# A transformer layer on one core: its last attention sequence, the step to the MLP, and the MLP's chain from bank to bank are rewritten

## The reference

```
cond = silu(c) @ wc.T + bc                    # split: sh1 sc1 g1 sh2 sc2 g2, one row of each per sequence
h = ln(x) * (1 + sc1) + sh1
q = h @ wq.T  (16 heads of 32)   k, v = h @ wk.T, h @ wv.T  (4 groups of 32)
a = softmax(q @ k.T / sqrt(32));  x = x + g1 * ((a @ v) @ wo.T)
h = ln(x) * (1 + sc2) + sh2
x = x + g2 * (gelu(h @ w1.T + b1) @ w2.T + b2)   # w1: 2048 x 512
```

## Time and profile before

| | us |
|---|---|
| three timed runs | 1500.55, 1500.60, 1503.28; median 1500.6 |
| profiled execution, its own time | 1506.23 |
| its span, first to last instruction | 1504.5 |
| mean granted clock of TensorE | 0.984 of full |
| busy in the span: TensorE, VectorE, ScalarE, GpSimd | 1447.9, 800.1, 621.3, 577.0 |

### The profile page before, as it was taken

The page is one execution under the profiler, slowest core; times in us unless marked ns, Lnnn a source line. Parts: engine busy times, 40 slices in busy tenths (PEclk is TensorE's granted clock), DMA queues, the critical chain, the costliest instruction groups (busy, mean ns, idle before and its releaser), DMA issues. The chain is left out here.

```text
span 1504.5 us, 19118 instructions
## 1 busy us (share of the span) xinstructions
PE 1447.9 (96%) x6989; PEld 1048.7 (70%) x6989; DVE 800.1 (53%) x1360; ACT 621.3 (41%) x1118; POOL 577.0 (38%) x224
## 2 busy tenths in 40 slices
PE   6899999999999999999799999999999999999996
PEld 5655666656666566655378878787887878878785
DVE  6877777776777677776334432424224242332421
ACT  6376657585766667575333212121121122112110
POOL 1067587776778586877200020202002020120202
PEclk9999999999999999999899999999999999999998
DMA  8232422323232324221342220200102010010100
GB/s 296 61 82 53 111 55 82 98 80 115 82 108 78 103 54 124 66 83 39 105 149 83 77 64 1 91 0 28 63 0 91 0 64 27 28 63 0 63 1 28
DMA packets 68388, 105.15 MB, mean 70 GB/s; under 512 B 10504, under 2 KB 19736, under 8 KB 68320
## 3 DMA queue, kind: packets, MB, share of 16 engines
q1 hardware_dynamic: 68320, 104.27, 22.6%
HBM read 55.44 MB, written 16.81 MB: 48 GB/s over the span
## 5 line engine op out<-in xcount | busy, mean ns | idle before, releaser
L824 DVE TENSOR_REDUCE neg_max<-row_bank 128x1 f32<-128x512 f32 x512 | 337.6, 683 | 146.8 <-PE row_bank L1062 142.3
L1500 PE MATMUL acc<-w_t,hidden 128*128 128x512 f32 x1536 | 370.8, 391 | 7.7 <-DVE hidden L1417 7.7
L1490 PE MATMUL up<-h,w_t 128*128 128x512 f32 x1536 | 371.2, 392 | 0.0
L668 ACT ACTIVATE probs<-key_bank 128x512 f32<-128x512 f32 x512 | 299.6, 597 | 169.1 <-PE key_bank L1075 163.8
L1500 PEld LDWEIGHTS acc<-w_t,hidden 128*128 128x128 f32 x1536 | 287.3, 188 | 69.9 <-DVE hidden L1417 10.7
L1490 PEld LDWEIGHTS up<-h,w_t 128*128 128x128 f32 x1536 | 287.6, 188 | 58.7
L1415 DVE CAST hidden<-gelu_full 128x512 fp32r<-128x512 f32 x128 | 67.4, 527 | 443.8 <-ACT gelu_full L1361 442.2
L1361 ACT ACTIVATE gelu_full<-up,bias_cols 128x512 f32<-128x512 f32 x128 | 88.3, 690 | 515.3 <-PE up L1490 515.3
L547 POOL TENSOR_TENSOR probs_sum<-probs_sum,probs 128x2048 f32<-128x2048 f32 x62 | 285.4, 4603 | 15.6 <-ACT probs L668 9.3
L1075 PE MATMUL key_bank<-q_stack,k_stack 98*128 98x512 f32 x512 | 221.3, 435 | 4.2 <-ACT probs L668 3.9
L1318 POOL TENSOR_TENSOR y<-y,gate_now 128x512 f32<-128x512 f32 x32 | 47.4, 1482 | 454.9 <-DVE y L1425 454.9
(11 more groups left out here) (133 smaller groups left out, 1066.0 us busy)
## 6 DMA issues: line engine op xcount, KB each, us to landing
q_stack<-spare SPq DMA_DIRECT2D x384, 64.0 KB, 2.0
xa<-in_x_dram SPq DMA_DIRECT2D x8, 1024.0 KB, 9.4
resid<-in_x_dram SPq DMA_DIRECT2D x8, 1024.0 KB, 7.0
x_scratch<-resid SPq DMA_DIRECT2D x8, 1024.0 KB, 4.5
xa<-x_scratch SPq DMA_DIRECT2D x8, 1024.0 KB, 5.8
spare<-in_L_cond_w_dram SPq DMA_DIRECT2D x32, 256.0 KB, 3.0
resid<-x_scratch SPq DMA_DIRECT2D x8, 1024.0 KB, 6.8
out_dram<-y SPq DMA_DIRECT2D x8, 1024.0 KB, 4.2
```

Source lines behind the costliest of these rows:

```text
L668: nc.scalar.activation(probs[kt][:, r, :], key_bank[r % 2][:, :], ACT.Exp).then_inc(exp_done, 1)
L824: nc.vector.tensor_reduce(out=neg_max[:, g % 2, i:i + 1], in_=row_bank[(g + i) % 2][:, :], op=ALU.max, axis=AX.X, negate=True).then_inc(ro ...
L1490: last = nc.tensor.matmul(up[j % 2][:, :], w1_t[i][:, kt, j * P:j * P + P], h[k][:, kt, :], start=(kt == 0 and n == 0), stop=(kt == KD - 1 ...
L1500: last = nc.tensor.matmul(acc[tt][:, :], hidden[j % 2][i][:, tt * P:tt * P + P], w2_t[k][:, j, :], start=(j == 0 and n == 0), stop=(j == N ...
```

## The change

1. **One block for both halves.** `attention` and `mlp` return their functions for each engine, and one block calls first the one, then the other. wq_t and wo_t move in memory.
2. **A table of its own for the last sequence** (`LAST_FILL`): O1d, O2 and O3 later, T0 to T3 at the ends of groups 0 and 3.
3. **Sums of the last sequence:** two additions in place of three; `sums` takes the fourth tile by a second set of matmuls. The groups' heads go into wq_t, which is free by then.
4. **The end of attention:** sums right after the products with V; O2 and O3 in the two `row_bank`s, all four tiles first for three groups, with weight tiles 0 and 1 turned between them (into `acc` banks, which are the former `key_bank`s); then the fourth group of all four. `up_product(0)` waits for two gates, `down_product(0)` for all.
5. **MLP in place:** Gelu and the modulation write back into their PSUM banks; ScalarE makes the high part, VectorE only the low one. up(j) now waits for the split of hidden j - 2, not its Gelu.
6. **The output:** VectorE multiplies `acc` by the gate; GpSimd has b2 times the gate added to the residual ahead of time, and adds that once. In the last sequence VectorE adds tiles 2 and 3 itself, and each tile is stored by its own transfer of 256 KB.
7. **The front:** B3 ahead of r0.

```diff
+WEIGHTS_AHEAD = 2
+LAST_FILL = {
+    (0, 0): ("Q3a", "Q3bc", "", "Q3d"),   (0, 1): ("", "", "VT", ""),
+    (0, 2): ("", "", "", ""),             (0, 3): ("", "", "T0", ""),
+    (1, 0): ("O0a", "O0b", "", "O0c"),    (1, 1): ("", "", "O0d", ""),
+    (1, 2): ("", "O1ab", "", ""),         (1, 3): ("O1c", "", "", ""),
+    (2, 0): ("", "O1d", "O2a", ""),       (2, 1): ("", "", "O2b", ""),
+    (2, 2): ("O2c", "O2d", "", ""),       (2, 3): ("", "O3a", "", "O3b"),
+    (3, 0): ("", "O3cd", "", "T1 T2"),    (3, 1): ("", "", "", ""),
+    (3, 2): ("T3", "", "", ""),           (3, 3): ("", "", "", ""),
+}
-... Wo.3 Mc3.1 Mc3.2 Mc3.3 r0 r1 Wc4.0 Q1a B3 r2 r3 Wc4.1 Mc4.0 r4 ...
+... Wo.3 Mc3.1 Mc3.2 Mc3.3 B3 r0 r1 Wc4.0 Q1a r2 r3 Wc4.1 Mc4.0 r4 ...
...
+def adds_in(b):
+    return TT - 2 if b == B - 1 else TT - 1
 # sums, TensorE
+summed = [probs_sum] + ([probs[TT - 1]] if adds_in(b) < TT - 1 else [])
+if len(summed) > 1:
+    pe.wait_ge(exp_done, exps_no(b, g, TT - 1) + R)
+for i, tile in enumerate(summed):
     for r in range(R):
-        last = nc.tensor.matmul(sum_bank[...], ones[:, :], probs_sum[:, r, :], start=True, stop=True)
+        last = nc.tensor.matmul(sum_bank[...], ones[:, :], tile[:, r, :], start=(i == 0), stop=(i == len(summed) - 1))
 # after, TensorE
 values(b, HKV - 1, TT - 2)
 values(b, HKV - 1, TT - 1)
-for tt in range(2):
-    out_part(b, tt, u, range(HKV - 1), True)
 sums(b, HKV - 1)
-for tt in range(2):
-    out_part(b, tt, u, range(HKV - 1, HKV), True)
-for tt in range(2, TT):
-    out_part(b, tt, u, range(HKV), True)
+for tt in range(TT):
+    if tt == 2:
+        pe.wait_ge(row_taken, row_no(b, HKV - 1, ROWS) + 1)
+    out_part(b, tt, u, range(HKV - 1), after_bank(tt))
+    if tt % 2 == 1:
+        turn_weights(pe, tt // 2)
+for tt in range(TT):
+    out_part(b, tt, u, range(HKV - 1, HKV), after_bank(tt))
 # after, ScalarE
 attn_high(b, HKV - 1)
+for j in range(WEIGHTS_AHEAD):
+    weights_high(act, j)
 # after, VectorE
 attn_low(b, HKV - 1)
+weights_low(dve, 0)
 for tt in range(TT):
+    if tt == 2:
+        weights_low(dve, 1)
     gate(b, tt, after_units(), after_bank(tt))
...
+def turn_bank(j, half):
+    return acc[half] if j < WEIGHTS_AHEAD else turn[half]
 # MLP, SP, first sequence
+for j in range(RING, RING + WEIGHTS_AHEAD):
+    load_ring(j)
+store_x1(sp, B - 1)
 sp.dma_start(b2_rows[:, :], ...)
 load_next(b, is_first)
-for j in range(RING, NJ):
+for j in range(RING + WEIGHTS_AHEAD, NJ):
 # MLP, SP, last store
+def store_tiles(b):
+    for tt in range(TT):
+        who, n = (y_added, b * TT + (tt + 1)) if tt < POOL_TILES else (y_added_last, tt - POOL_TILES + 1)
+        sp.wait_ge(who, n)
+        sp.dma_start(out[b, tt * P:tt * P + P, :], y[:, tt, :]).then_inc(out_stored, 16)
+    sp.wait_ge(out_stored, b * 16 + TT * 16)
 # MLP, GpSimd
+def bias_resid(b, is_first):
+    pool.wait_ge(gate_loaded, b * 16 + 16)
+    nc.gpsimd.tensor_tensor(gated_b2[:, :], b2_rows[:, :], gate_now[:, :], ALU.mult).then_inc(b2_gated, 1)
+    pool.wait_ge(resid_loaded, b * 16 + 16)
+    for tt in range(TT):
+        nc.gpsimd.tensor_tensor(resid[:, tt, :], resid[:, tt, :], gated_b2[:, :], ALU.add).then_inc(resid_biased, 1)
-for tt in range(TT):
+for tt in range(TT if has_next else POOL_TILES):
     pool.wait_ge(acc_taken, n)
-    nc.gpsimd.tensor_tensor(y[:, tt, :], y[:, tt, :], gate_now[:, :], ALU.mult).then_inc(y_gated, 1)
     nc.gpsimd.tensor_tensor(y[:, tt, :], y[:, tt, :], resid[:, tt, :], ALU.add).then_inc(y_added, 1)
 # MLP, ScalarE, step j
+if has_next and j == NJ - 1:
+    for kt in range(2):
+        h_high(b, kt)          # Copy of the turn bank into h[0]; the first waits for up_ready of step 15
-nc.scalar.activation(gelu_full[j % 2][:, :], up[j % 2][:, :], ACT.Gelu, ...)
+nc.scalar.activation(up[j % 2][:, :], up[j % 2][:, :], ACT.Gelu, ...)
+nc.scalar.activation(hidden[j % 2][0][:, :], up[j % 2][:, :], ACT.Copy).then_inc(hid_hi, 1)
+if has_next and j == NJ - 1:
+    for kt in range(2, KD):
+        modulate_next(b, kt)
+        h_high(b, kt)
 # MLP, VectorE, step j
-nc.vector.tensor_copy(hidden[j % 2][0][:, :], gelu_full[j % 2][:, :]).then_inc(hid_hi, 1)
-nc.vector.tensor_tensor(hidden[j % 2][1][:, :], gelu_full[j % 2][:, :], as_f32(hidden[j % 2][0][:, :]), ALU.subtract)
+nc.vector.tensor_tensor(hidden[j % 2][1][:, :], up[j % 2][:, :], as_f32(hidden[j % 2][0][:, :]), ALU.subtract)
 # take_acc, VectorE
-nc.vector.tensor_tensor(y[:, tt, :], acc[tt][:, :], b2_rows[:, :], ALU.add).then_inc(acc_taken, 1)
+nc.vector.tensor_tensor(y[:, tt, :], acc[tt][:, :], gate_now[:, :], ALU.mult).then_inc(acc_taken, 1)
+def add_last(b, tt):           # last sequence, tiles 2 and 3
+    nc.vector.tensor_tensor(y[:, tt, :], y[:, tt, :], resid[:, tt, :], ALU.add).then_inc(y_added_last, 1)
 # MLP, TensorE
-    pe.wait_ge(h_ready, b * KD + (kt - 1))
+    pe.wait_ge(h_split, b * KD + (kt - 1))
+if is_first and j == 0:
+    pe.wait_ge(banks_taken, banks_count - 2)     # ahead of up_product(0); banks_count ahead of down_product(0)
-    pe.wait_ge(gelu_done, b * NJ + (j - 1))
+    pe.wait_ge(hid_split, b * NJ + (j - 1))
```

More of the change, by code:

```diff
@@ L56 @@
     (3, 3): ("", "Vd", "", ""),
+}
+LAST_FILL = {
+    (0, 0): ("Q3a", "Q3bc", "", "Q3d"),
+    (0, 1): ("", "", "VT", ""),
+    (0, 2): ("", "", "", ""),
+    (0, 3): ("", "", "T0", ""),
+    (1, 0): ("O0a", "O0b", "", "O0c"),
+    (1, 1): ("", "", "O0d", ""),
+    (1, 2): ("", "O1ab", "", ""),
+    (1, 3): ("O1c", "", "", ""),
+    (2, 0): ("", "O1d", "O2a", ""),
+    (2, 1): ("", "", "O2b", ""),
+    (2, 2): ("O2c", "O2d", "", ""),
+    (2, 3): ("", "O3a", "", "O3b"),
+    (3, 0): ("", "O3cd", "", "T1 T2"),
+    (3, 1): ("", "", "", ""),
+    (3, 2): ("T3", "", "", ""),
+    (3, 3): ("", "", "", ""),
 }
@@ new lines, in layer_kernel, with _ @@
+        second, turn_weights, weights_high, weights_low = mlp(nc, f32, f32r, ALU, ACT, sb, ps, sem, as_f32, seq_dram, ident, cond_cols, bias_cols, neg_half, norm_bufs,
+                     spare, resid, gate_now, gated, store_x1, x1_stored, banks_taken, banks_count, w_loaded, load_weights, b2, x1_dram, gate_dram, out)
+        with nc.Block() as block:
+            @block.sync
+            def _(sp):
+                first[0](sp)
+                second[0](sp)
+            @block.gpsimd
+            def _(pool):
+                first[1](pool)
+                second[1](pool)
+            @block.scalar
+            def _(act):
+                first[2](act, weights_high)
+                second[2](act)
+            @block.vector
+            def _(dve):
+                first[3](dve, weights_low)
+                second[3](dve)
+            @block.tensor
+            def _(pe):
+                first[4](pe, turn_weights)
+                second[4](pe)
@@ new lines, in sequence, with after @@
+                    stack_max(b + 1, 0)
+                if has_last:
+                    store_x1(sp, b - 1)
+            def after(b):
+                for g in range(HKV):
+                    sp.wait_ge(k_stacked[g], b * STACKED + STACKED)
+                    for i in range(2):
+                        sp.wait_ge(q_stacked[i][g], queries_stacked(b, 2))
+                load_resid(b)
+                for j in range(RING):
+                    load_weights(sp, j)
+            before()
+            sequence(0, False, True)
```

1905 lines of the change are left out of this document (954 added, 951 removed).

## The result

| | before | after |
|---|---|---|
| median of the timed runs, us | 1501.94 (4 runs, 1500.55 to 1503.93) | 1466.74 (4 runs, 1464.45 to 1467.79) |
| profiled execution, span, us | 1504.5 | 1462.7 |
| mean granted clock | 0.984 | 0.996 |

The ratio is 0.9763, 95% interval 0.9744 to 0.9781: 32.9 to 38.4 us faster, 35.2 between the medians. The forecast was -32.8 us and 1467.8. To see where, I cut both at the same five instructions, by their starts in the timeline: the first score, the first score of the last sequence, the first product with V behind the last score, up(1), and down(15) of the last sequence.

A forecast was written before the change was run, and what follows sets the result against it. TensorE, busy 96% of the span, was taken as the bound, so only its idle, waiting or half-clock time pays. -0.3 - 3.7 - 13.8 - 7.7 - 7.3 = -32.8 us from 1500.6 gave 1467.8, range 1459 to 1478.

The forecast's parts named there:

- From the last scores to up(1), -13.8: Step from attention to MLP: 33.96 us falls to 20.1 with the last head's chain covered by matmuls, -13.8 us.
- bound of -10.4: Smallest gain for the step to up(1): one stretch of 6.8 us stays at half clock, 3.4 us.
- The MLP, -7.7: MLP in place in PSUM: down(0)'s wait of 1.10 us goes at 7 changes of sequence; bounds -7.7 to -4.9 us.
- The spare time before down(15): MLP, change of sequence: the new chain ends at 947.7, down(15)'s weights load at 947.95, 0.25 us to spare.
- rival 3: A new wait replaces the removed one, at down(15) or at up(0) for gates; 1470.5 to 1473.3, up to 1475; 9%.
- 65 ns: Skill's extra VectorE cost of a PSUM access over SBUF; by it down(15)'s 0.25 us to spare would be 0.19.
- The last sequence, -3.7: Last attention sequence: idle time stays, half clock goes, 78.75 to 75.05 us; bounds -8.4 to +3.0.
- Rival 2: Half clock stays in the last sequence, group 0 being sparse; term 0 to +3.0, time 1471.5 to 1474.5 us; 20%.
- It only makes room: Last sequence: dropping GpSimd's third addition frees nothing itself, but sums don't come to wait when the group gets shorter.
- The tail, -7.3: After TensorE's end: shared additions and a last store of 256 KB end at 1496.8, not 1504.1; bounds -8.3 to -5.5.
- The front, -0.3: B3 earlier: the 1.16 us wait before Mc4.0 is mostly exchanged for another; bounds -1.9 to +1.4 us.
- I am wrong if: Refuting signs: VectorE or ScalarE releasing before down(15), the clock dropping in group 0, or new sums waiting for additions.

The follow-up runs named there:

- e3: Changed kernel with B3 back behind r1 and Wc4.0 in the front; timed 1466.17 us.
- e4: Changed kernel with VectorE instead of ScalarE making the rounded high part of hidden, cast out of PSUM; timed 1467.72 us.
- e11: Changed kernel with T0 to T3 of the last sequence back in group 0, the quarters of O as in the new table; timed 1469.28 us.
- e6: Changed kernel with the old order of parts at the end of attention, one block and the new banks kept; timed 1473.01 us.
- e8: Changed kernel with attention and MLP in two blocks again; timed 1471.97 us.
- e9: Changed kernel with the old MLP chain (Gelu into SBUF, VectorE's cast and subtraction out of SBUF), new output kept; timed 1476.86 us.
- e2: Changed kernel with three additions and one set of sums in the last sequence, new table kept; timed 1472.30 us.
- a0_after: The changed kernel itself run once more, unedited, as reference; timed 1466.11 us.
- e10: Changed kernel with GpSimd adding the residual to all four tiles of the last sequence, VectorE none; timed 1466.28 us.
- e5: Kernel before, with GpSimd's two operations on each output tile left out (output without gate and residual); timed 1485.47 us.

## Why the prediction was right, step by step

- **From the last scores to up(1), -13.8: right.** 20.1 us were forecast, 19.95 and 20.43 measured in the two profiles of the changed kernel, with every cover that was named: no row of that stretch has a wait. Over the seven edits that leave this step alone it took 19.97 to 21.67; the longest, in e3, e4 and e11, hold a stretch at half clock, for which the bound of -10.4 had room. e6 and e8 show that both the order and the single block are needed, at 6 to 8 us each.
- **The MLP, -7.7: mechanism right, size too small, measured -10.0.** The step that was off is "Wait gone, 7 x 1.10 = 7.7 us", and -7.7 was also the larger bound. The 1.10 us are the idle time between the modelled end of one matmul and the start of the next. From start to start up(0) and up(1) took 6.70 us before down(0) (950.80 to 957.50) and 5.44 after (926.24 to 931.68), which is 1.26; and the dozen behind the wait took 2.87 instead of 2.72, since its weights could not be loaded ahead. 1.26 + 0.15 = 1.41, times 7 is 9.9. The trace held both numbers. The spare time before down(15), forecast 0.25, is 0.21, so rival 3 did not come. The comparison of 0.68 us from PSUM with 0.80 from SBUF, by which the prediction set its 65 ns aside, had the slowed subtractions in the 0.80; the medians of the subtraction for hidden are 0.693 us out of SBUF before and 0.692 out of PSUM after, so what it concluded stands.
- **The last sequence, -3.7: right, measured -3.3 to -5.2 in the profile.** The reason given holds: idle time stays (4.4 for 4.65 us), the half clock goes, and TensorE is busy for 69.6 us where 70.4 were forecast. But the half clock doesn't go in every execution. Of the nine profiles of kernels whose last sequence is that of the changed kernel, six take 73.6 to 74.0 us, and three 75.3 to 75.5, with a stretch at half clock in group 3 (e3, e4) or group 1 (e9). Rival 2, which had group 0 losing its clock, did not come in group 0 in any of them. What I had not seen is how much the freed GpSimd matters: "It only makes room" was the right sentence, but e2 shows that without it group 2 takes 6 us more.
- **The tail, -7.3: mechanism right, size too small, measured -8.7.** Three terms are off. VectorE's last addition ended 4.4 us after its first product, not 5.0. From there to the end of the span are 2.6 us, not 3.1: the store was priced by the load of 256 KB, 3.0 us, and lands in 2.1. And the end before was taken as 1504.1 where the span ends at 1504.45. Tile 2 waits for GpSimd (1.29 us for it, 0.68 for tile 3), as the prediction had it from the Trainium skill (SBUF — State Buffer, Who interferes with whom).
- **The front, -0.3: B3 is worth 0 at the first score (e3), and the term missed what shortened the front.** The exchange of one wait for the other is what the list shows: TensorE gains 0.3 us up to Mc4.0, where its lead on the kernel before goes from 0.4 to 0.7 us (48.09 for 48.80), and loses it at the row maxima. The profiled front is 2.4 us shorter all the same, beyond the bound of -1.9. The largest part is the half clock at 50 us: the lead goes from 0.7 to 2.4 us over it (51.50 for 53.92). The 0.4 us before it are left of 0.85 us that arise at 11 us: eight transposes take 1.04 us there (from 11.03 in the timeline) where they took 1.86 before (from 11.10). The granted clock is listed as 1.00 in both, so why stays open; in the other profiles of the changed kernel and its edits they take 1.04 to 1.91.
- **The sum: inside the range, but too small by 2 to 7 us, and the nearness of 1467.8 is in part luck.** The terms of the profile add up to -41.8, mine to -32.8; the timed medians differ by 35.2 (first comparison) and 36.8 (with a0_after), and the two estimates with e3 and e10 are 38.0 and 39.5. Four of the five terms lie beyond their own bounds, all on the side of the larger gain: the front, the step to up(1) (by 0.2 us), the MLP and the tail. The forecast of 1467.8 is only 1.1 us from the measured 1466.74 because it started from 1500.6, which is lower than all later medians of the kernel before (1501.94 to 1505.76). The rest of the 41.8 is the choice of executions: before in a slow one, after in its fastest. That slower executions of the kernel before spent more time at half clock, the timed runs bear out: of the 21 in the three sets, the 13 with a mean granted clock of 0.986 or more have a median of 1502.1 us, the 8 with 0.985 or less 1505.9. Where in the kernel that time lies no timed run shows.
- **The signs.** No "I am wrong if" came: nothing stands as releaser before down(15), the clock stays up in group 0, and the sums wait for no addition. Two signs of being right did not come as stated. Groups 1 and 3 take 20.95 and 15.85 us, not 16 to 20; the idle time of group 1 is a single wait of 1.6 us for row maxima. And from TensorE's end to the end of the span are 5.1 us, not 6.5.

## What to carry to other kernels

Price a wait by the distance of the starts around it, the weight loads behind it included, not by the idle time in the list. Look at what the other engine on SBUF does at the moment of a slow VectorE instruction: taking its operand out of PSUM may be worth more than taking the instruction away. Where a stretch is made denser so that the clock stays up, look at once which engine is the next bound in the shorter stretch; here neither the table nor the additions shortened the sequence without the other.

## What was not expected of the hardware

The stretches at half clock need not fall at the same place in two executions of the same program: the changed kernel had one at 17.5 to 24.4 us and one at 72 in one profile, one at 22.4 and one at 111 to 118 in the other, and the time of sequences 0 to 6 went from 574.1 to 576.0 us over its relatives with no edit there. But they can: before and e5, which share their attention, had all seven within 0.2 us of each other. The cast of 128x512 takes 0.43 us out of SBUF when GpSimd is idle (all 128 in e5), 0.68 to 0.69 out of PSUM whether GpSimd works or not (all 128 in e4), and up to 1.51 out of SBUF when GpSimd works (before).
